# A graph network kernel on one core: counts at five units per four units of sums, and all thirteen blocks in the run plan

## The reference, cut to what matters

```
layer 0: msg = sum over 8 bases of (x[src] @ weight[b]) * w_comp[etype, b], times edge_weight
         agg = segment_sum(msg, dst);  x1 = layernorm(x + relu(agg + bias))
layer 1: neigh = segment_sum(x1[src] + edge_attr, dst)
         h = ((1 + eps) * x1 + neigh) @ W1 + b1;  h = relu(batchnorm(h));  out = h @ W2 + b2
         result = layernorm(x1 + out)
```

## Time and profile before

| what | value |
|---|---|
| median of three executions | 666.05 us |
| profiled execution, its own time | 670.06 us |
| span of the profiled execution | 668.2 us |
| mean granted TensorE clock | 0.872 |
| busy: PE, DVE, POOL, ACT | 82%, 73%, 62%, 45% |
| DRAM traffic over the span | 161 GB/s |

### The profile page before, as it was taken

How to read it: one execution, slowest core, us unless ns; L and a number is a source line. 1 busy time by engine, 2 the same in 40 slices (tenths; PEclk the granted TensorE clock), 3 DMA queues, 4 the chain that set the end, 5 groups by cost and what they waited for, 6 DMA issues and landing times.

```text
span 668.2 us, 13132 instructions
## 1 busy us (share of the span) xinstructions
PE 545.4 (82%) x3874; PEld 439.0 (66%) x3874; DVE 488.7 (73%) x1852; ACT 303.5 (45%) x689; POOL 414.0 (62%) x434
## 2 busy tenths in 40 slices
PE   4779777877798868888797889598986999999774
PEld 3569676567685757766786758586765887767231
DVE  6998988679976678884798856988648883541535
ACT  9736545464442544533544435344434452100656
POOL 6777777777777777777777777777777740000000
PEclk9978769787787869897789879798979899999977
DMA  5424667555756366584566656757747469700003
GB/s 129 117 53 126 190 182 192 170 136 166 222 158 205 112 175 204 163 248 138 171 184 194 213 164 199 216 165 245 236 107 241 123 183 366 281 1 2 0 10 89
DMA packets 96220, 108.21 MB, mean 162 GB/s; under 512 B 10757, under 2 KB 80630, under 8 KB 96146
## 3 DMA queue, kind: packets, MB, share of 16 engines
q1 hardware_dynamic: 80082, 79.25, 38.0%
q0 software_dynamic: 13312, 27.29, 15.2%
q10 hardware_dynamic: 2752, 0.79, 0.6%
HBM read 81.73 MB, written 25.56 MB: 161 GB/s over the span
## 4 chain that ended last, share of the span: by engine, by line
PE 38%; DVE 25%; POOL 13%; issue 9%; DMA 5%; ACT 5%; DVEq 3%; SPq 1%; ACTq 0%
POOL gathered_flat L707 13%; PE psum L1041 12%; PE psum L1016 7%; PE psum L986 7%; DVE etype_hot L1370 5%; PE psum L992 4%; DVE sums_flat L1479 4%; PE psum L1007 4%; DVE etype_hot L1367 3%; DVE weighted L1291 3%; DVE adj_flat L1455 2%; DVE adj_flat L1267 2%; DMA gathered_flat<-in_x_dram,src_i 2%; DMA adjacency<-adj_flat 2%; PE psum L1176 1%
## 5 line engine op out<-in xcount | busy, mean ns | idle before, releaser
L707 POOL DMA_INDIRECT gathered_flat<-in_x_dram,src_i x416 | 411.7, 990 | 129.1 <-issue 123.1
L986 PE MATMUL psum<-weighted,gathered_flat 128*128 128x160 f32 (+1 forms) x832 | 162.7, 326 | 38.4 <-DMA gathered_flat<-in_x_dram,src_i 16.3
L986 PEld LDWEIGHTS psum<-weighted,gathered_flat 128*128 128x128 f32 x832 | 145.6, 224 | 54.8 <-issue 34.6
L794 ACT ACTIVATE gathered_flat<-psum 128x25 f16<-128x25 f32 x182 | 35.0, 192 | 238.2 <-PE psum L1007 231.6
L1370 DVE TENSOR_SCALAR etype_hot<-iota_key,key_t 128x300 f16<-128x300 f16 (+1 forms) x416 | 134.1, 324 | 0.0
L1479 DVE TENSOR_TENSOR sums_flat<-psum,sums_flat 128x180 f32 x208 | 71.6, 344 | 84.3 <-PE psum L992 56.2
L770 ACT ACTIVATE adj_flat<-zero_col 128x450 f16<-128x450 f32 x208 | 107.9, 574 | 42.3 <-DMA adjacency<-adj_flat 31.9
L992 PEld LDWEIGHTS psum<-hot,attrs 128*128 128x128 f32 x832 | 126.2, 217 | 0.0
L992 PE MATMUL psum<-hot,attrs 128*128 128x20 f32 (+1 forms) x832 | 121.7, 263 | 0.0
L1007 PE MATMUL psum<-etype_hot 128*128 128x300 f16 (+2 forms) x624 | 108.7, 286 | 0.0
L796 ACT ACTIVATE adj_flat<-psum 128x475 f32 x182 | 107.3, 590 | 0.2 <-issue 0.2
(11 more groups left out here) (143 smaller groups left out, 356.4 us busy)
## 6 DMA issues: line engine op xcount, KB each, us to landing
attrs<-in_edge_attr_dram SPq DMA_DIRECT2D x51, 512.0 KB
adjacency<-adj_flat SPq DMA_DIRECT2D x26, 900.0 KB, 4.9
gathered_flat<-in_x_dram,src_i POOLq DMA_INDIRECT x416
sums_flat<-adjacency SPq DMA_DIRECT2D x11, 576.0 KB, 6.5
coef<-adjacency SPq DMA_DIRECT2D x20, 288.0 KB, 6.7
sums_flat<-adjacency SPq DMA_DIRECT2D x6, 648.0 KB, 7.6
sums_flat<-adjacency SPq DMA_DIRECT2D x10, 288.0 KB, 6.4
etype_hot<-adjacency SPq DMA_DIRECT2D x1, 1656.0 KB, 10.3
```

The source lines that it names most:

```text
L707: pool.indirect_dma_start(gathered[:, t % (RING * GROUP), :], None, x[:, :], bass.IndirectOffsetOnAxis(src_i[:, t:t + 1], 0)).then_inc(gat ...
L986: nc.tensor.matmul(ps[:, 0:B, STARTS[i]:STARTS[i] + WIDTHS[i]], gathered[:, (u * UNIT + i) % (RING * GROUP), 0:F], weighted_tiles(s, i)[:, ...
```

## The change

Counts no longer go one unit behind the sums. With counted(u) = min(208, 5(u + 1)/4 rounded down), PE after the sums of unit u does the counts from counted(u - 1) to counted(u), so every fourth unit has two. Counts are complete at unit 166, and units 167 to 207 have none. ACT's copies follow the same rule, DVE builds keys six units ahead of counted, and adds the shared columns of counts up to counted(2w - 1) at couple w. The offsets of the shared columns are read into registers by their own groups of four. A pair is stored in the group in which its counts are complete (store_step).

Block 12 is planned like the others. By the planner's rules there are now 45 runs instead of 41, with 696 matmuls instead of 624; up to couple 83 they have 432 instead of 372. After the loop come seven fills (84 matmuls instead of 96) and thirteen finals of 15 (195 instead of 255). The special buffers and loads of block 12 go; its rest takes the place of the keys.

Inside a chunk, the steps stand later: turn_back at unit + 6 (before + 5), the residual at couple + 4 (+ 3), the deviations at unit + 11 (+ 9), the norm at couple + 6 (+ 5), turn_norm at unit + 15 (+ 13), the copy of x1 at unit + 16 (+ 14), the own term at couple + 9 (+ 8). FIRST is unchanged.

```diff
@@ -91,7 +91,15 @@
     def done_unit(k):
         return -(-(k + 1) * CHUNK * E // (N * UNIT * P)) + 2
+    def counted(u):
+        return max(0, min(U, 5 * (u + 1) // 4))
+
+    def store_step(p):
+        couple = min(w for w in range(COUPLES + 1) if counted(2 * w - 1) >= (p + 1) * PU)
+        return couple // 2
+
     FIRST = [-(-(done_unit(k) + 4) // 2) * 2 for k in range(LOOPED)]
+    BACK_AT, ROOT_AT, TURN_AT, KEEP_AT = 6, 11, 15, 16
     STRIDE = done_unit(1) - done_unit(0)
     assert FIRST[-1] + 20 < U and all(done_unit(k) == done_unit(0) + k * STRIDE for k in range(LOOPED))
@@ -101,10 +109,10 @@
     LEAD = 3
     def split_step(k):
-        return (FIRST[k] // 2 + 8) // 2
+        return (FIRST[k] // 2 + 9) // 2
     def block_step(b):
-        return BLOCK * PAIR * b + (5 if b < BLOCKS - 2 else 4)
+        return store_step(BLOCK * b + BLOCK - 1) + 2
     def places_for(chunks):
         places = [(i, split_step(chunks - 1)) for i in range(NEARS)]
@@ -115,11 +123,11 @@
     def plan_runs():
-        runs, reached, used = [], [0] * (BLOCKS - 1), {}
+        runs, reached, used = [], [0] * BLOCKS, {}
         for w in range(COUPLES):
-            held = any(first - 2 <= 2 * w + 1 <= first + 15 for first in FIRST)
-            ready = sum(2 * w >= first + 16 for first in FIRST)
-            best = max((min(2, ready - reached[b]) if w >= 2 * block_step(b) + (5 if b < BLOCKS - 2 else 6) else 0, -b) for b in range(BLOCKS - 1))
+            held = any(first - 2 <= 2 * w + 1 <= first + KEEP_AT + 1 for first in FIRST)
+            ready = sum(2 * w >= first + KEEP_AT + 2 for first in FIRST)
+            best = max((min(2, ready - reached[b]) if w >= 2 * block_step(b) + 5 else 0, -b) for b in range(BLOCKS))
             if held and w % 2:
                 continue
             for chunks in range(best[0], 0, -1):
...
@@ -625,16 +629,13 @@
                     if g == GROUPS - 1:
                         for k, _ in LATE_CHUNKS:
                             load_rows_of_x(k)
-                        for b in LOAD_ORDER[0:6]:
+                        for b in LOAD_ORDER[0:6] + LOAD_ORDER[12:13]:
                             load_last(b)
-                    if g % PAIR == PAIR - 1:
-                        store_adjacency(g // PAIR)
-                for b in LOAD_ORDER[6:]:
+                    for p in range(PAIRS):
+                        if store_step(p) == g:
+                            store_adjacency(p)
+                for b in LOAD_ORDER[6:12]:
                     load_last(b)
-                sp.wait_ge(counts_mm, U)
-                stored(BLOCKS - 1)
-                sp.dma_start(row_buffer, counts_of(BLOCKS - 1, 0, ROW_TILES)).then_inc(row_in, 16)
-                sp.dma_start(row_rest, counts_of(BLOCKS - 1, ROW_TILES, HIGHS)).then_inc(row_in, 16)
             with sp.Else():
                 def load_attr(t, rows):
                     wait_alone(sp, wide_tile[0], t + 1)
@@ -820,19 +821,20 @@
                 for j in range(GROUP):
                     zero_adjacency(0, j)
                 for u in range(U):
-                    p, j = u // PU, u % PU
-                    copy_counts(u)
-                    if p + 1 < PAIRS and j >= PU // 2:
-                        if j == PU // 2 and p >= 1:
-                            act.wait_ge(adj_out[(p + 1) % 2], 16 * ((p + 1) // 2))
-                        for i in range(2):
-                            zero_adjacency((p + 1) % 2, 2 * j - PU + i)
+                    for c in range(counted(u - 1), counted(u)):
+                        p, j = c // PU, c % PU
+                        copy_counts(c)
+                        if p + 1 < PAIRS and j >= PU // 2:
+                            if j == PU // 2 and p >= 1:
+                                act.wait_ge(adj_out[(p + 1) % 2], 16 * ((p + 1) // 2))
+                            for i in range(2):
+                                zero_adjacency((p + 1) % 2, 2 * j - PU + i)
                     for k in range(LOOPED):
                         if u == FIRST[k] + 4:
                             keep_agg(k, CHUNK)
-                        if u == FIRST[k] + 9:
+                        if u == FIRST[k] + ROOT_AT:
                             chunk_deviations(k, CHUNK)
-                        if u == FIRST[k] + 14:
+                        if u == FIRST[k] + KEEP_AT:
                             keep_x1_columns(k, CHUNK)
                 for k, n in LATE_CHUNKS:
                     keep_agg(k, n)
@@ -1063,8 +1065,8 @@
                 pe.wait_ge(weights_in, 16 * 12)
                 for u in range(U):
                     sums_of_unit(u)
-                    if u:
-                        counts_of_unit(u - 1)
+                    for c in range(counted(u - 1), counted(u)):
+                        counts_of_unit(c)
                     for k in range(LOOPED):
                         step = u - FIRST[k]
                         if step == 0:
...
@@ -1454,22 +1451,28 @@
                     shared = pair_counts(p)[:, :, bass.ds(share, 1)]
                     nc.vector.tensor_tensor(shared, side[:, u % SIDES, :].unsqueeze(2), shared, ALU.add).then_inc(counts_added, 1)
-                waiting = []
+                def group_values(g, h, top):
+                    return nc.values_load_multi_w_load_instructions(
+                        base_row[0:1, g, h, :], engines=(ENGINE.DVE,), min_val=0, max_val=top,
+                        skip_runtime_bounds_check_because="the flag says so")[1]
+
+                shares = {}
                 for w in range(COUPLES):
                     g = 2 * w // GU
                     if w % 2 == 0:
-                        places = nc.values_load_multi_w_load_instructions(
-                            base_row[0:1, g, :, :].rearrange("p h j -> p (h j)"), engines=(ENGINE.DVE,), min_val=0,
-                            max_val=N - 1, skip_runtime_bounds_check_because="bases are node numbers")[1]
-                        shares = [nc.s_assert_within(place, 0, SPREAD - WIN, skip_runtime_bounds_check_because=
-                                                     "the flag says so") for place in places[GU:2 * GU]]
+                        places = group_values(g, 0, N - 1)
+                    ripe = range(counted(2 * w - 3), counted(2 * w - 1))
+                    for c in ripe:
+                        if c // GU not in shares:
+                            shares = {h: shares[h] for h in shares if h + 1 == c // GU}
+                            shares[c // GU] = group_values(c // GU, 1, SPREAD - WIN)
                     if w - 1 in RUN_AT:
                         firsts = block_bases(RUNS[RUN_AT[w - 1]][1])
                     dve.wait_ge(sums_mm, w + 1)
                     if runs_before(w - 1) > runs_before(w - 2):
                         dve.wait_ge(nbr_added, BLOCK * runs_before(w - 1))
                     for k in range(LOOPED):
-                        if w == FIRST[k] // 2 + 9:
+                        if w == FIRST[k] // 2 + 10:
                             dve.wait_ge(own_added, k + 1)
                     for j in range(2):
                         u = 2 * w + j
@@ -1477,26 +1480,24 @@
                         if u:
                             dve.wait_ge(added, u)
                         nc.vector.tensor_tensor(window, unit_psum(u), window, ALU.add).then_inc(added, 1)
-                    for u in (2 * w + KEYRING - 1, 2 * w + KEYRING):
-                        if u < U:
-                            keys_hot(u)
+                    for c in range(min(U, counted(2 * w - 2) + KEYRING), min(U, counted(2 * w) + KEYRING)):
+                        keys_hot(c)
                     if w - 1 in RUN_AT:
                         n = RUN_AT[w - 1]
                         dve.wait_ge(added, 2 * w + 2)
                         add_block(n, run_bank(n), firsts)
-                    for u, share in waiting:
-                        if u % PU:
-                            shared_column(u, share)
-                    waiting = [(2 * w + j, shares[(2 * w + j) % GU]) for j in range(2)]
+                    for c in ripe:
+                        if c % PU:
+                            shared_column(c, shares[c // GU][c % GU])
                     for k in range(LOOPED):
-                        if w == FIRST[k] // 2 + 3:
+                        if w == FIRST[k] // 2 + 4:
                             chunk_residual(k, CHUNK)
-                        if w == FIRST[k] // 2 + 5:
+                        if w == FIRST[k] // 2 + 6:
                             chunk_norm(k, CHUNK)
                             chunk_split(k, CHUNK, 0)
-                        if w == FIRST[k] // 2 + 6:
+                        if w == FIRST[k] // 2 + 7:
                             chunk_split(k, CHUNK, 1)
-                        if w == FIRST[k] // 2 + 8:
+                        if w == FIRST[k] // 2 + 9:
                             dve.wait_ge(added, 2 * w + 2)
```

(23 more changed lines are left out.)

## The result

The changed kernel takes **699.29 us** (median of four, 693.47 to 703.15), the kernel before 666.86 in the same runs: a ratio of 1.047 [1.042, 1.052]. The forecast was slower, by 5 us; it is slower by 32, and outside the range of 653 to 689 us.

The account below looks back on a forecast made before the run. POOL's gathers were taken to pace the loop as a whole, DVE its start, PE its end. Terms of +45, -28.5 and -11.3 us summed to +5, forecasting 671 us against 666.05; range for 8 in 10, 653 to 689 us.

Parts of the forecast that it names:

- B: Couples 84 to 103, on PE: with no counts left there, 77 us instead of 105.5, so -28.5 us.
- C: After the loop, on PE: fewer finals and fills, a shorter last run and no counts of unit 207, -11.3 us.
- my 0.6 us a couple: In A, up to 126 us: next to no waits for PE, so the whole added cost of 0.6 us a couple stands.
- the ring of counts: In A: ACT's wait for a pair's store before zeroing is passed on once in full, +5 us (0 to 13).
- a rival with 0.14: The ring of counts binds: ACT's 4.41 us wait passed on at four pairs of 25, +18 instead of +5, 684 us; chance 0.14.
- A: Couples 0 to 83, on DVE, 405.8 us before: the added work, less absorbed waits, plus the ring, gives +45 us.
- the stores' new place in SyncE's queue: SyncE issues stores in the step whose counts are complete; none is added, so priced at nothing.
- The absorbed term: In A: added work fills part of DVE's 44.0 us of waits for PE, -20 us (-7 to -40).
- 60 for DVE's work: In A, on DVE: 42 more counts +50.4, four more runs +4.8, register reads +4.0, one more set of keys +0.8 us.
- The steps at nothing: Later steps in a chunk remove PE's wait for ACT before turn_back but cost and give DVE nothing.
- The clock: More counts in A could keep PE's clock fast through chunk starts, 7 us less of DVE's waits, making 664 us.
- the places of couples 83 and 103: Sign of a right forecast: DVE adds couple 83 near 499 us and couple 103 near 576 us.

Follow-up runs that it names:

- f1: The changed kernel without zeroing from the third pair on, waiting for the store only before a pair's first copy: 664.24 us, 0.997 of the kernel before.
- f0: The changed kernel run again, unedited, against the kernel before: 700.01 us against 665.99, ratio 1.052.
- h2: The changed kernel with a chunk's steps at their earlier places, against the kernel before: 707.63 us, ratio 1.062.
- h1: The kernel before without zeroing from the third pair on and with the store wait four counts later: 664.49 us against 666.97, ratio 0.998.
- e2: The same kernel as h1, on a chip where the kernel before is slow: 797.02 us, ratio 0.996.

## Why the prediction was wrong

- **The forecast's sign and two of its three terms held.** B: -28.5 forecast, -27.4 measured; PE is busy 76.8 of 78 us. C: -11.3 forecast; -10.8 measured. The first 20 couples took 92.8 us after 78.5 (couple 20 is added at 141.8), +14.3, and my 0.6 us a couple gives 12. But that agreement is luck: in f1 they took 86.4, +7.9, so some 6 of the 14 us are the ring's.
- **The step that failed is the price of the ring of counts: +5 taken, 0 to 13 as the range, 36 measured** (f0 against f1). The mechanism was named, as a term and as a rival with 0.14, and its price of 18 us was half of what the ring costs. I read the bound from the earlier trace rows: DVE's gaps of 0.22 us beside ACT's wait of 4.41. That row is from four couples a pair. At 3.2 couples DVE also adds the shared columns in the couple after PE has made them, so the line from last copy to landed store got longer while the pair got shorter: from last copy to store 8.4 us in the mean over A, against 5.8, and from store to landing 5.9 against 4.9 (medians). Both changes were in my text; I didn't add them up. I had also priced the stores' new place in SyncE's queue at nothing, and two of them were held back there for over 5 us; their share of the 36 us stays open. The rest of the sum held: without its ring term it gives +0.2 us, and f1 measured -1.8.
- **The absorbed term was near once the ring is relieved.** I took 20 us of DVE's 44 us of waits for PE as filled. In f1 they are 19.8, so 24 went. With the ring bound they grew to 52.5 instead: a wait of ACT passed to PE comes back to DVE as waiting. The two terms were not independent, and I had added them as if they were. With the ring relieved A is +32.6 us (f1); my sum without its ring term was +40, with 60 for DVE's work. In the change's own trace that work is 40.7 us of busy time and 11 of small gaps. Part of the difference is a wrong count: DVE builds keys ahead, so only 37 of the 42 added units of keys fall into A. So A's miss of 22 us is some 29 us too little for the ring, less 7 us too many for the rest.
- **The steps at nothing**: they save about 7 us (h2, its changed plan included). With the early steps PE waits 10.1 us for ACT before turn_back (line 1026) instead of 4.3, and 72.0 instead of 61.4 for ACT's copies (f0).
- **The clock** explains nothing of the miss: 0.84 was granted over A before and after, so the way to 664 us by a faster clock in A did not open. In B it rose from 0.92 to 1.00, where PE is busy nearly all the time; my sum for B was built from rows at full clock.
- Of the signs I named, the last gather after 550 (590.7), POOL waiting for PE (51.1 us; f1, with 14.4, is near the 15 I forecast), no PE wait for gathered rows and finals of 26 us (26.7 after 34.0) came. DVE over 85% busy did not (78% from 48 to 440 us), nor waits for PE under 30 us (52.5), nor the places of couples 83 and 103. The named mark for the ring, couple 83 later than 510 and over 60 us at line 770, is what was found (521.6 and 148).

## What to carry to other kernels

Before work is pushed through a ring faster, add up the line that frees a slot (last write, the other engine's part, store, clearing) and compare it with the new time per slot; an engine that is 45% busy can still hold the loop. A wait that costs nothing at the present rate says nothing of its slack. What worked here needed neither more buffer nor less work, but another order: the neighbour's part one unit sooner, the wait later in the waiting engine's queue, and a lower rate.

## What the runs showed of the hardware

The kernel before took 666 to 667 us in three sets of runs and 802 to 813 on three other chips. h1's kernel has a trace from both kinds (h1 and e2), with the same operations: 96,218 DMA packets in each, a gather 0.94 us at the least in each. The difference is idle time in every engine; for ACT and DVE most of it is laid to releasers outside the core's engines (remote). The waits of e2 over the whole span:

```profile
ACT gathered_flat L796 <- remote: 176.1, 45, 7.9
...
DVE sums_flat L1479 <- remote: 106.8, 44, 4.6
...
POOL gathered_flat L707 <- remote: 61.8, 40, 2.2
...
DVE adj_flat L1267 <- remote: 25.0, 1, 25.0
```

Setup alone ended 30 us later (first add at 77.9 instead of 48.3 us), while PE ran single matmuls some 2 us apart. No run tested why, and the cause stays open.
